# GNN edge layer: edge features and their one-hot brought turned into the first layer's operand, in place of turning them on the chip

## The reference

```python
m_input = concatenate([x[src], x[dst], edge_attr_64], axis=-1)   # 100000 x (128 + 128 + 64)
h = relu(m_input @ W1 + b1)
messages = relu(h @ W2 + b2)
agg = segment_sum(messages, dst)                                  # 3125 x 128
x = layernorm(x + layer_norm(x + relu(agg @ Wn + bn)) )
```

## Time and profile before

| | value |
|---|---|
| median of 3 runs | 1711.21 us |
| profiled execution | 1713.62 us |
| its span | 1711.5 us |
| PE busy | 1455.2 us, 85% |
| GpSimd busy | 778.2 us, 45% |
| DVE busy | 760.2 us, 44% |
| ScalarE busy | 668.1 us, 39% |
| HBM traffic | 87.44 MB read, 6.52 MB written |

### The profile page before, as it was taken

How to read it: one execution, slowest core, us unless ns; L and a number is a source line. 1 busy time by engine, 2 the same in 40 slices (tenths; PEclk the granted TensorE clock), 3 DMA queues, 4 the chain that set the end, 5 groups by cost and what they waited for, 6 DMA issues and landing times.

```text
span 1711.5 us, 31298 instructions
## 1 busy us (share of the span) xinstructions
PE 1455.2 (85%) x9660; PEld 1036.9 (61%) x9773; DVE 760.2 (44%) x2782; ACT 668.1 (39%) x1236; POOL 778.2 (45%) x818
## 2 busy tenths in 40 slices
PE   1689999989976877788898888889898889887997
PEld 0346666755555656666676667666666667654554
DVE  9987888632233322243334233323433343345445
ACT  4765555520002434353435334433443344331113
POOL 3300000000005777777777777777777777711000
PEclk9999999999987999999999999999999989988999
DMA  2000000001015333333333333333333333300001
GB/s 67 1 0 1 2 1 2 22 7 39 1 46 132 96 82 82 80 86 83 83 79 89 79 82 78 92 79 82 87 83 82 80 87 83 82 23 3 1 1 38
DMA packets 158117, 95.16 MB, mean 56 GB/s; under 512 B 119959, under 2 KB 143422, under 8 KB 158030
## 3 DMA queue, kind: packets, MB, share of 16 engines
q0 software_dynamic: 25024, 51.25, 11.7%
q1 hardware_dynamic: 133006, 42.78, 10.2%
HBM read 87.44 MB, written 6.52 MB: 55 GB/s over the span
## 4 chain that ended last, share of the span: by engine, by line
PE 30%; DMA 12%; POOL 10%; issue 8%; DVE 5%; DVEq 2%; ACT 1%; SPq 1%; POOLq 0%; ACTq 0%
POOL arena L733 10%; DMA arena<-x_w1a,idx 10%; PE ps L1175 6%; PE ps L1060 6%; PE ps L1069 5%; PE ps L1053 4%; PE ps L1049 3%; PE ps L1041 3%; PE ps L1110 1%; PE ps L1159 1%; DVEq L334 1%; DVE arena L2029 1%; DVE idx L1996 1%; DMA x_w1b<-arena 1%; DVE stats L2043 1%
## 5 line engine op out<-in xcount | busy, mean ns | idle before, releaser
L733 POOL DMA_INDIRECT arena<-x_w1a,idx x780 | 738.0, 946 | 680.9 <-issue 636.5
L1491 ACT ACTIVATE arena<-ps 88x512 f32<-88x512 f32 x196 | 116.2, 593 | 480.5 <-PE ps L1041 474.0
L1069 PEld LDWEIGHTS ps<-arena 128*128 128x128 f32 x1568 | 208.4, 195 | 109.0 <-issue 75.4
L1049 PE MATMUL ps<-ident_f,arena 128*128 128x128 f32 x784 | 130.6, 291 | 115.3 <-DMA arena<-x_w1a,idx 114.9
L2029 DVE TENSOR_TENSOR arena<-ps,bias_b 128x512 f32<-128x512 f32 x196 | 135.5, 692 | 205.8 <-PE ps L1060 205.8
L2024 DVE TENSOR_TENSOR arena<-win_i,late 128x96 f32<-128x96 f32 x196 | 51.1, 260 | 393.9 <-PE ps L1069 386.1
L1311 ACT ACTIVATE adj<-ps 128x300 f32 x392 | 172.0, 449 | 138.3 <-PE ps L798 131.3
L1060 PE MATMUL ps<-w_c,arena 128*128 128x128 f32 x1568 | 221.7, 288 | 0.0
L793 PE MATMUL ps<-arena 128*128 128x300 bf16 x784 | 167.5, 296 | 57.6 <-DVE arena L1769 54.7
L1053 PE MATMUL ps<-arena 88*128 88x512 f32 x392 | 207.9, 612 | 1.8 <-ACT arena L1491 1.8
L1060 PEld LDWEIGHTS ps<-w_c,arena 128*128 128x128 f32 x1568 | 205.0, 204 | 0.3
(11 more groups left out here) (199 smaller groups left out, 1415.2 us busy)
## 6 DMA issues: line engine op xcount, KB each, us to landing
arena<-in_edge_attr SPq DMA_DIRECT2D x196, 128.0 KB, 2.5
arena<-x_w1a,idx POOLq DMA_INDIRECT x782
arena<-x_w1b SPq DMA_DIRECT2D x196, 12.0 KB
x_spill<-arena SPq DMA_DIRECT2D x1, 1600.0 KB, 7.2
x_w1a<-arena SPq DMA_DIRECT2D x6, 256.0 KB, 2.3
x_w1b<-arena SPq DMA_DIRECT2D x6, 256.0 KB, 2.4
arena<-x_spill SPq DMA_DIRECT2D x6, 256.0 KB, 3.0
out_x<-arena SPq DMA_DIRECT2D x3, 512.0 KB
```

Of the source, the lines that this page charges most:

```text
L733: pool.indirect_dma_start(out=z_e[v][:, j * D:(j + 1) * D], out_offset=None, in_=xa_d[:, :], in_offset=bass.IndirectOffsetOnAxis(ap=idx[:, ...
L1049: pe.matmul(z_t[:, j * P:(j + 1) * P], z_e[v][:, j * P:(j + 1) * P], ident_f[:, :], is_transpose=True, start=(j == 0), stop=False)
L1069: last = pe.matmul(ps[:, WIN_BANK[v % 2], 0:WIN], msg[:, j * P:(j + 1) * P], oh_e[v][:, j, :], start=(j == 0), stop=(j == J - 1))
```

## The change

The host hands over the edge features turned (`attr_turned`, 64 x edges) and the edges' targets as one row of int32 (`dst_numbers`). Per block SP loads the features straight into rows 0 to 63 of `ec_t` (now two buffers, v % 2), and broadcasts the 512 targets to rows 64 to 87 (two DMAs, both waiting for `z_ready` of two blocks before). DVE turns the latter in place into the one-hot: row 64 + w becomes 1.0 where the target equals base + w (`onehot_turned`, a tensor_scalar with one number per partition, taken from `first_nodes`, which is computed once before the stage). `ec`, `inputs_t`, `inputs_out` and their semaphores go, and one of the two comparisons in `block_start`. `onehot_turned` of v+2 stands on DVE behind `block_start` of v+3 and before `add_bias` of v; PE waits for it before line 1053. `hidden_relu` now waits for `z_ready` by itself. The projections' buffer and `msg` move in the arena. Of the diff, without unchanged lines and without renames of buffers and call sites:

```diff
@@ -92,7 +92,9 @@
-        base_row = sb("base_row", [1, NB], I32)
+        node_numbers = sb("node_numbers", [P, NB], I32)
+        base_row = node_numbers[0:1, :]
+        first_nodes = node_numbers[R:R + WIN, :].bitcast(F32)
@@ -159,13 +162,11 @@
         def edge(a, n):
-        ec = [edge(J * KE * u, J * KE).rearrange("p (j f) -> p j f", j=J) for u in range(2)]
-        o = 2 * J * KE
+        ec_t = [edge(512 * u, 512) for u in range(2)]
+        o = 1024
-        msg = edge(o + 2560, 512)
-        assert o + 3072 <= 3776
-        ec_t = edge(8000, 512)
+        msg = edge(8000, 512)
@@ -535,10 +534,11 @@
             def features(i, v):
-                passed(sp, ec_used, i, v, back=2)
-                sp.dma_start(ec[v % 2][:, :, 0:R],
-                             t["edge_attr_64"][bass.ds(e0, BLK), :].rearrange("(j p) f -> p j f", p=P)
+                passed(sp, z_ready, i, v, back=2)
+                sp.dma_start(ec_t[v % 2][R:KE, :].bitcast(I32),
+                             t["dst_numbers"][bass.ds(e0, BLK)].rearrange("(a e) -> a e", a=1).broadcast_to([WIN, BLK])
+                sp.dma_start(ec_t[v % 2][0:R, :], t["attr_turned"][:, bass.ds(e0, BLK)]).then_inc(ec_loaded[v], 16)
@@ -664,6 +664,8 @@
+            g.add(pool.iota(part_i[:, :], pattern=[[0, 1]], base=-R, channel_multiplier=1,
+                            allow_small_or_imprecise_dtypes=True))
@@ -1032,15 +1034,6 @@
-            def inputs_t(i, v, first=False):
-                passed(pe, ec_loaded, i, v, by=16)
-                if first:
-                    passed(pe, ec_onehot, i, v)
-                    passed(pe, ect_out, i, v, back=1)
-                for j in range(J):
-                    last = pe.transpose(ps[0:KE, 0, j * P:(j + 1) * P], ec[v % 2][:, j, :], ident_f[:, :])
-                last.then_inc(ec_used[v], 1)
-
             def hidden_t(i, v):
@@ -1048,9 +1041,9 @@
-                passed(pe, ect_out, i, v)
+                passed(pe, ec_onehot, i, v)
-                pe.matmul(z_t, w_e[v % 2][0:KE, :], ec_t[0:KE, :], start=False, stop=True
+                pe.matmul(z_t, w_e[v % 2][0:KE, :], ec_t[v % 2][0:KE, :], start=False, stop=True
             def messages(i, v, first=False):
@@ -1485,14 +1474,8 @@
-            def inputs_out(i, v):
-                passed(act, ec_used, i, v)
-                passed(act, z_ready, i, v, back=1)
-                act.activation(ec_t[0:KE, :], ps[0:KE, 0, :], ACT.Copy).then_inc(ect_out[v], 1)
-
-            def hidden_relu(i, v, first=False):
-                if first:
-                    passed(act, z_ready, i, v)
+            def hidden_relu(i, v):
+                passed(act, z_ready, i, v)
@@ -1501,8 +1484,6 @@
             def step(i, v, left=2):
-                if left >= 2:
-                    inputs_out(*at(i, v + 2))
@@ -1999,6 +1978,7 @@
+            own.add(dve.tensor_scalar(first_nodes, base_all[R:KE, :], part_i[R:KE, 0:1], None, ALU.add))
@@ -2014,15 +1994,18 @@
-            def block_start(i, v, first=False):
-
-                if first:
-                    passed(dve, ec_used, i, v, back=2)
+            def block_start(i, v):
+
-                dve.tensor_tensor(ec[v % 2][:, :, R:KE], w, rel, ALU.is_equal).then_inc(ec_onehot[v], 1)
+
+            def onehot_turned(i, v):
+                passed(dve, ec_loaded, i, v, by=32)
+                rows = ec_t[v % 2][R:KE, :]
+                dve.tensor_scalar(rows, rows.bitcast(I32), first_nodes[:, bass.ds(SLOTS * i + v, 1)], None,
+                                  ALU.is_equal).then_inc(ec_onehot[v], 1)
             def add_bias(i, v):
@@ -2109,14 +2092,16 @@
-            def step(i, v, b=None, left=3, first=False):
+            def step(i, v, b=None, left=3):
-                    block_start(*at(i, v + 3), first)
+                    block_start(*at(i, v + 3))
+                if left >= 2:
+                    onehot_turned(*at(i, v + 2))
@@ -2512,7 +2499,8 @@
-        "edge_attr_64": _np.pad(_np.asarray(inputs["edge_attr_64"]), ((0, PAD), (0, 0))),
+        "dst_numbers": _np.pad(dst, (0, PAD), constant_values=-1),
+        "attr_turned": _np.pad(_np.asarray(inputs["edge_attr_64"]).T, ((0, 0), (0, PAD))),
```

More of the change, by code:

```diff
@@ L107, in build @@
         std_deg = sb("std_deg", [P, NT], F32)
+        part_i = sb("part_i", [P, 1], F32)
         stats = sb("stats", [P, CH * 2, 6], F32)
@@ L259, in build @@
         ec_onehot = [sem(f"ec_onehot{v}") for v in range(SLOTS)]
-        ec_used = [sem(f"ec_used{v}") for v in range(SLOTS)]
         w_loaded = [sem(f"w_loaded{v}") for v in range(SLOTS)]
         oh_e_ready = [sem(f"oh_e_ready{v}") for v in range(SLOTS)]
-        ect_out = [sem(f"ect_out{v}") for v in range(SLOTS)]
         z_ready = [sem(f"z_ready{v}") for v in range(SLOTS)]
@@ L359, in proj @@
         def proj(n):
-            return arena[:, 2752 + 512 * (n % 2):3264 + 512 * (n % 2)]
+            return arena[:, 3072 + 512 * (n % 2):3584 + 512 * (n % 2)]
         def stores(h, u):
@@ L1079, in step @@
                     sum_nodes(*at(i, v - 1))
-                if left >= 2:
-                    inputs_t(*at(i, v + 2), first)
                 messages(i, v, first)
@@ L1205, in _ @@
             with pe.Else():
-                inputs_t(0, 0, first=True)
-                inputs_t(0, 1, first=True)
                 hidden_t(0, 0)
@@ L1656, in _ @@
             with act.Else():
-                inputs_out(0, 0)
-                inputs_out(0, 1)
-                hidden_relu(0, 0, first=True)
+                hidden_relu(0, 0)
                 for v in range(SLOTS + 1):
@@ L2360, in _ @@
                 for v in range(3):
-                    block_start(0, v, first=True)
+                    block_start(0, v)
+                for v in range(2):
+                    onehot_turned(0, v)
                 dve.memset(agg_all, 0.0).then_inc(agg_zero, 1)
                 dve.wait_ge(agg_zero, 1)
-                step(0, 0, first=True)
+                step(0, 0)
                 step(0, 1)
```

## The result

The changed kernel takes 1717.45 us at the median of ten runs (1714.96 to 1719.32), the kernel before 1711.28 us; ratio 1.0034, interval [1.0024, 1.0044]. So it is slower by about 6 us, in the forecast direction and inside the range, but a quarter of the forecast 25 us. Its profiled execution took 1716.95 us with a span of 1714.7; before, 1713.62 and 1711.5. Single executions of one kernel differ by 5 us, so the spans alone say little, and I read what lies inside them.

The account below looks back on a forecast made before the run. GpSimd's gathers were taken as the bound, 5.0 us a block. Profiled 1713.6 us + 0.4 at the start + 25 in the loop - 1 = 1738.0; 2.4 lower for the median, 1735.6, forecast 1736 us, range 1709 to 1750.

Parts of the forecast that it names:

- The bound: Edge stage: GpSimd's gathers set the pace, 5.0 us a block, 980 us over 196 blocks; removing PE's transposes gains 0 us.
- PE busy about 1335 us: Sign that the forecast is right: PE's busy time after the change, with 121 us of transposes removed.
- The distance between gathers: Sign in the edge stage: 1.28 us on average from one gather to the next, where it was 1.252.
- The start: Start of the edge stage: two more SP issues, +1.14 us, and a GpSimd stall that goes, -0.73 us; sum +0.4 us.
- The duration of the comparison: New DVE comparison, 24 partitions x 512: 0.43 us, with bounds 0.29 and 0.55 us.
- The exclusion between comparison and gather: Edge loop: a one-input DVE operation and a GpSimd instruction exclude each other; in a gather, the last part, about 0.57 to 0.94 us.
- the 26.4 us term of the sum: Edge loop: in 91 steps the comparison ends inside a gather's last part and GpSimd loses 0.17, 0.27 or 0.37 us each.
- 25 - 1: Edge loop: 25 us lost by gathers to the new comparison, 1 us back from the removed two-input comparison.
- rival 1: Edge loop: not slower, GpSimd gives way to nobody late in its gather or the comparison always waits; 1711.6 us, chance 0.30.
- a lock over the whole gather: Edge loop: the comparison gets ahead only between two gathers, some 11 of 195 steps, 3 us; 1714.5 us, chance 0.10.
- the place: Edge loop: the comparison's start is fixed relative to the gathers, 0.26 us after line 2024's present start.
- Rival 4: Edge stage: PE with less load falls to 1.2 GHz, 7.4 us a block; 470 us more if the clock stays low; chance 0.03.

## Why the prediction was right or wrong, point by point

- The bound: right. GpSimd's gathers set the edge stage, 1.25 us apart whatever PE does; the runs with three gathers show it. Removing the transposes gave nothing. Two readings under it were wrong: PE's part of a block is 3.68 us and not 4.33, since the durations overlap, and the sign "PE busy about 1335 us" did not come (1463.0), since the lower clock took up what was removed; nor did PE's wait for the gathers grow by 0.62 us a block (114.9 to 124.1 us in all). Neither changes the bound. The distance between gathers, forecast as 1.28 us, is 1.261.
- The start: wrong in its parts. The two more issues of SP cost nothing that can be seen: from the first copy of projections to the first gather it is 16.99 us before (510.37 to 527.36) and 16.93 us after (508.50 to 525.43). The stall of GpSimd did not vanish; in the profiled execution it is 2.23 us of idle time where it was 1.03, and 0.98 to 2.21 us in runs with the same start. The sum, about +1 in place of +0.4 us, hardly matters.
- The duration of the comparison: 0.48 us undisturbed, where I took 0.43; right within its bounds.
- The exclusion between comparison and gather: right. Both directions occur, and both parts of a gather are exposed.
- The step that failed is the size of a stretch, the 26.4 us term of the sum. I took the whole recorded operation, or all but 0.1 us of it, as the time for which GpSimd is kept out: 0.17 to 0.37 us for each of 91 blocks. The traces show at most 0.12 us in the late part and 0.24 us at a gather's start. A comparison that starts at 0.51 us isn't ahead, it waits. Those that wait end 0.25 us after the gather, where an undisturbed one lasts 0.48; read so, a comparison takes what it needs only some 0.23 us after its start, and one that starts at 0.35 us and costs nothing must give it back before its end. 26.4 us became 1.5 in that part, and 3.5 us came at the gathers' starts, where I had 2 to 4.5. In all, the gathers' sum rose by 5.7 us where I had 25 - 1, and the two inputs of the removed comparison gave back at most 0.8. The measured 1717.45 us lies nearer to rival 1 (1711.6, or 1714.5 with a lock over the whole gather) than to 1736, though neither form of that rival is what the rows show: comparisons do get ahead in the middle of a gather, and little is lost by it.
- The second part of that step, the place, was wrong as well: not fixed at 0.0 to 0.4 us as in the kernel before, but spread over the gather. That PE's lower clock spreads it was only argued; it didn't decide, since with the load put back the gathers' sum was no less (744.7 us).
- Rival 4 (the clock): I gave it 0.03 and said that a PE that is always busy gets its clock back. In the changed kernel it gets it back in part (0.61 in 600 to 630 us, 0.85 in 560 to 1300), and GpSimd has no wait from it; with the one-hot a little later it stays at 0.50 for at least 170 us though busy for 9.0 to 9.6 of every 10 us, and the kernel takes 71 us more than the changed one. My price of 7.4 us a block came from durations that overlap; the block measured there takes 6.8. The premise, that less load lowers the clock, is shown. Whether any of the 6 us goes through the clock is open: the run with ScalarE's one-hot wins about 3 us back by PE work alone, but the changed kernel wins nothing by the same work (1.0039 for 1.0034). By the times of the runs with four columns and with ScalarE, about half of the 6 us is the comparison's; the other half is not placed.
- The Trainium skill, SBUF - State Buffer, section "Who interferes with whom", has the two-input operation contend only with GpSimd's reads and the two-port one with all. The traces fit the first: the comparison with two inputs stretched the gathers' starts alone, by up to 0.5 us; that the start is where a gather reads isn't shown by any run. For the two-port mode the section says: "Whoever issues first gets the shared pair for the whole instruction". That is not what the rows show: a comparison that starts 0.01 us into a gather runs beside it and neither is longer, and in the late part an operation of 0.48 us keeps a gather out for 0.12 us at most.

## What to carry to other kernels

Find the engine whose instructions follow each other at a constant distance, whatever the chain of waits says; work taken from any other engine gives nothing, and what is added beside it is priced by how long it keeps that engine out of what they share, which is less than the instruction's duration. When work is taken from PE, read its granted clock after: PE's busy time can stay nearly where it was, and with a new wait in each step it can stay low and become the bound.

## What the runs showed of the hardware that I had not expected

- A PE that is busy 9.0 to 9.6 of every 10 us can stay at 1.2 GHz for at least 170 us (590 to 760 us, comparison behind the addition); four useless transposes a block lift it to 0.96 on average and the kernel from 1788.67 to 1723.78 us.
- With ScalarE's one-hot, 776 PE instructions fewer (9764 to 8988) and no less PE busy time: 1465.4 us with the useless transposes at a clock of 0.95 in 560 to 1300 us, 1466.9 without them at 0.85.
- A one-input DVE operation of 0.48 us keeps a gather of 0.94 us out for at most 0.12 us in its late part and 0.24 us at its start; a two-input one of 0.68 us for up to 0.5 us at the start and not in the late part.
